# Attention in a two-block transformer kernel: projections cut in contraction halves and spread between the score blocks

## What is computed

```python
q = x @ Wq.T + bq + ocr_bias
k = x @ Wk.T + bk
v = x @ Wv.T + bv                      # 16 heads of 16 features each
scores = einsum('bhsd,bhtd->bhst', q, k) / sqrt(16)
scores = scores + band_mask            # 0.1 where |s - t| <= 2
attn = softmax(scores, axis=-1)
out = einsum('bhst,bhtd->bhsd', attn, v)
return out @ Wo.T + bo
```

## Time and profile before

| | us |
|---|---|
| median of 3 runs (lowest, highest) | 4187.68 (4182.49, 4190.27) |
| the profiled execution's own time | 4184.78 |
| its span, first to last instruction | 4183.0 |
| PE busy in the span | 3742.0 |
| attention loop, first to last first-pass maximum | 2157.3 to 3386.0 |

### The profile page before, as it was taken

One profiled execution on the slowest core, in us unless ns is written; L12 is line 12 of the kernel. 1 busy time (PEld: TensorE's weight loads), 2 busy tenths in 40 slices (PEclk: granted clock), 3 DMA queues, 4 the chain that ended last, 5 costly groups with the idle time before them and its releaser, 6 DMA issues. The chain is left out here.

```text
span 4183.0 us, 80084 instructions
## 1 busy us (share of the span) xinstructions
PE 3742.0 (89%) x27516; PEld 2902.7 (69%) x27516; DVE 2700.8 (65%) x5625; ACT 1772.3 (42%) x3205; POOL 1377.5 (33%) x1049
## 2 busy tenths in 40 slices
PE   6997788887997999999948998999998969999999
PEld 4886677776887888888824544555555538888888
DVE  5665677775666566666656666666666645666665
ACT  3444344443554333333325555555555553333333
POOL 2665222222665222222332333333323322222222
PEclk9999999998999899999969999999999989999999
DMA  3000000000001000000023323323323310000000
GB/s 102 0 0 14 2 0 0 0 0 1 0 0 38 1 0 0 0 0 0 1 72 88 88 68 87 87 68 88 86 68 91 83 46 6 15 10 10 15 10 16
DMA packets 92753, 131.72 MB, mean 31 GB/s; under 512 B 9824, under 2 KB 42992, under 8 KB 92672
## 3 DMA queue, kind: packets, MB, share of 16 engines
q1 hardware_dynamic: 90624, 130.13, 11.6%
q10 hardware_dynamic: 2048, 0.53, 0.1%
HBM read 71.38 MB, written 58.72 MB: 31 GB/s over the span
## 5 line engine op out<-in xcount | busy, mean ns | idle before, releaser
L1496 DVE TENSOR_REDUCE neg_max_sb<-s_ps 128x1 f32<-128x512 f32 x1024 | 667.3, 685 | 425.6 <-PE s_ps L1220 423.4
L1386 ACT ACTIVATE prob_sb<-s_ps 128x512 f32<-128x512 f32 x1024 | 575.0, 598 | 438.2 <-PE s_ps L1232 428.7
L850 POOL TENSOR_TENSOR m_act_lo_sb<-m_act_sb,m_act_hi_sb 128x512 fp32r<-128x512 f32 x320 | 414.2, 1295 | 1042.6 <-ACT m_act_hi_sb L816 1042.6
L806 ACT ACTIVATE m_silu_sb<-moe_h_ps 128x512 f32<-128x512 f32 x320 | 191.4, 598 | 967.4 <-PE moe_h_ps L761 967.4
L1138 POOL TENSOR_TENSOR prob_sb<-prob_sb,band_sb 128x520 f32<-128x520 f32 (+1 forms) x256 | 285.3, 1115 | 810.2 <-ACT prob_sb L1386 810.0
L904 DVE TENSOR_TENSOR m_act_sb<-moe_h_ps,m_silu_sb 128x512 f32<-128x512 f32 x320 | 220.6, 689 | 502.3 <-ACT m_silu_sb L806 472.7
L1232 PE MATMUL s_ps<-q_stack_sb,k_stack_sb 128*128 128x512 f32 x1024 | 409.1, 459 | 51.0 <-ACT prob_sb L1386 50.0
L529 POOL TENSOR_TENSOR f_sq_lo_sb<-f_sq_sb,f_sq_hi_sb 128x512 fp32r<-128x512 f32 x256 | 329.5, 1295 | 348.6 <-ACT f_sq_hi_sb L504 348.6
L1220 PE MATMUL s_ps<-k_stack_sb,q_stack_sb 96*128 96x512 f32 x1024 | 369.9, 430 | 71.7 <-DMA k_stack_sb<-qk_scratch 52.0
L916 DVE SCALAR_TENSOR_TENSOR x_resident_sb<-moe_y_ps,gates_sb,x_resident_sb 128x256 f32 (+1 forms) x1024 | 422.7, 475 | 0.5
L1232 PEld LDWEIGHTS s_ps<-q_stack_sb,k_stack_sb 128*128 128x128 f32 x1024 | 171.2, 191 | 359.5 <-ACT prob_sb L1386 212.3
(11 more groups left out here) (285 smaller groups left out, 8891.3 us busy)
## 6 DMA issues: line engine op xcount, KB each, us to landing
qk_scratch<-qk_hi_sb SPq DMA_DIRECT2D x128, 256.0 KB
q_stack_sb<-qk_scratch SPq DMA_DIRECT2D x128, 192.0 KB, 4.0
k_stack_sb<-qk_scratch SPq DMA_DIRECT2D x128, 192.0 KB, 4.2
qk_scratch<-qk_lo_sb SPq DMA_DIRECT2D x64, 256.0 KB
x_resident_sb<-x SPq DMA_DIRECT2D x4, 2048.0 KB, 17.7
out<-x_resident_sb SPq DMA_DIRECT2D x16, 512.0 KB
moe_w_values_sb<-routed_w SPq DMA_DIRECT2D x12, 512.0 KB, 6.5
q_stack_sb<-neg_max_t_sb ACTq DMA_DIRECT2D x128, 4.0 KB
```

The source lines that it names most:

```text
L850: nc.gpsimd.tensor_tensor(al[:, slot(e), :], act_f[:, e % 2, :], as_f32(ah[:, slot(e), :]), ALU.subtract).then_inc(low_ready, 1)
L1386: nc.scalar.activation(prob[:, kt % 2, i, :], s2p[i % 2][:, :], ACT.Exp).then_inc(exp_done, 1)
L1496: nc.vector.tensor_reduce(nm[:, g % 2, 2 * (i % 2) + i // 2, qt:qt + 1], s1p[n % 2][:, :], AXIS_X, ALU.max, negate=True).then_inc(max_done, 1)
```

## The change

The projections of tokens (v and the output) are cut in contraction halves: a piece is now three matmuls of 256 columns, so the tables have eight entries for each instead of four. All tables are rewritten, with the entries of DVE, ACT and POOL that follow from them: q and k of m = 1 are made at steps 5 and 6 instead of 8 and 9, the turning of the output goes from step 6 to step 7, the output projection from steps 10 and 11 to steps 8 to 11, the v projection from steps 13 to 15 to steps 12 to 15. `full` has a slice for each m, so m = 1 need not wait for `low_part` of m = 0. To make room, the spread value bias takes the place of `oh` and `ol`, which are used later. The number of instructions is the same. Score passes stay in blocks of two.

```diff
 XT_AT = [(1, 2), (2, 1)]
-QK_AT = [[(3, 2), (4, 0), (4, 1), (4, 2)], [(8, 0), (8, 1), (8, 2), (9, 0)]]
-OT_AT = [(6, 1), (6, 2)]
-Y_AT = [(10, 0), (10, 1), (10, 2), (11, 0)]
-V_AT = [(13, 2), (14, 1), (15, 0), (15, 2)]
+QK_AT = [[(3, 1), (3, 2), (4, 0), (4, 1)], [(5, 0), (5, 2), (6, 1), (6, 2)]]
+OT_AT = [(7, 0), (7, 1)]
+Y_AT = [(8, 1), (8, 2), (9, 0), (9, 2), (10, 1), (10, 2), (11, 0), (11, 1)]
+V_AT = [(12, 1), (12, 2), (13, 0), (13, 2), (14, 1), (14, 2), (15, 0), (15, 1)]
...
-        full = core.sbuf("qk_full", [P, 2, TOKENS], F32, ctx)
+        full = core.sbuf("qk_full", [P, KT, 2, TOKENS], F32, ctx)
...
-                        if more and st in (4, 9):
-                            low_part(b + 1, st // 8)
+                        if more and st in (4, 6):
+                            low_part(b + 1, int(st == 6))
...
-                def qk_proj(b, m, parts=range(4), after_o=False):
+                def qk_proj(b, m, parts=range(4)):
...
-                        if after_o:
-                            pe.wait_ge(ol_ready, b - 1)
...
-                def tokens(t, xh, xl, n, done):
-
-                    for k in range(KT):
-                        for i, (x, w) in enumerate([(xh, wh), (xh, wl), (xl, wh)]):
-                            op = nc.tensor.matmul(tpy[:, t, :], x[:, k, t * P:(t + 1) * P], w[n][:, k, :],
-                                                  start=(k == 0 and i == 0), stop=(k == KT - 1 and i == 2))
-                    if t == TILES - 1:
+                def tokens(piece, xh, xl, n, done):
+
+                    t, k = piece // KT, piece % KT
+                    for i, (x, w) in enumerate([(xh, wh), (xh, wl), (xl, wh)]):
+                        op = nc.tensor.matmul(tpy[:, t, :], x[:, k, t * P:(t + 1) * P], w[n][:, k, :],
+                                              start=(k == 0 and i == 0), stop=(k == KT - 1 and i == 2))
+                    if piece == TILES * KT - 1:
                         op.then_inc(done, 1)
...
-                                qk_proj(b + 1, 1, range(n, n + 1), before)
+                                qk_proj(b + 1, 1, range(n, n + 1))
                             if before and at in OT_AT:
                                 if more:
-                                    o_transpose(b - 1, OT_AT.index(at), full_ready, 2 * (KT * b + KT + 1))
+                                    o_transpose(b - 1, OT_AT.index(at), full_ready, 2 * (KT * b + 2 * KT))
...
-                    if not first(b) or m == 1:
-                        act.wait_ge(qkl_ready, KT * b + m)
-                    nc.scalar.activation(full[:, 1, :], tp[:, 1, :], ACT.Identity, bias=bk[:, m:m + 1]).then_inc(full_ready, 1)
+                    if not first(b):
+                        act.wait_ge(qkl_ready, KT * b + m - 1)
+                    nc.scalar.activation(full[:, m, 1, :], tp[:, 1, :], ACT.Identity, bias=bk[:, m:m + 1]).then_inc(full_ready, 1)
...
-                            if more and (st, i) in ((4, 3), (9, 1)):
-                                k_full(b + 1, st // 8)
+                            if more and (st, i) in ((4, 2), (6, 3)):
+                                k_full(b + 1, int(st == 6))
...
-                            if more and (st, i) in ((5, 1), (5, 2), (9, 2), (9, 3)):
-                                high_part(b + 1, st // 8, int((st, i) in ((5, 2), (9, 3))))
-                            if before and (st, i) in ((6, 3), (7, 0)):
-                                o_high(b - 1, st - 6)
+                            if more and (st, i) in ((4, 3), (5, 0), (7, 0), (7, 1)):
+                                high_part(b + 1, int(st == 7), int((st, i) in ((5, 0), (7, 1))))
+                            if before and (st, i) in ((7, 2), (7, 3)):
+                                o_high(b - 1, i - 2)
...
-                            if st % TILES == 2 and i == 3:
-                                if st > 2:
+                            if st % TILES == 3 and i == 2:
+                                if st > 3:
                                     normalise_out(b, st // TILES - 1)
...
-                            if more and (st, i) in ((4, 3), (9, 1)):
-                                q_full(b + 1, st // 8)
-                            if before and st == 7 and i in (0, 1):
-                                o_low(b - 1, i)
+                            if more and (st, i) in ((4, 2), (6, 3)):
+                                q_full(b + 1, int(st == 6))
+                            if before and (st, i) in ((7, 3), (8, 0)):
+                                o_low(b - 1, st - 7)
```

More of the change, by code:

```diff
@@ L1003, in att_stage @@
         oh, ol = (core.sbuf(n, [P, KT, TOKENS], F32R, ctx) for n in ("oh", "ol"))
-        ys = full[:, :, :].rearrange("p k (u d) -> p (k u) d", u=2)
+        bvs, bvl = oh[:, :, 0:P], ol[:, :, 0:P]
+        ys = full[:, 0, :, :].rearrange("p k (u d) -> p (k u) d", u=2)
         s1p = [core.psum(f"s1_{i}", [P, TOKENS], ctx) for i in range(2)]
@@ L1277, in o_transpose, with o_project @@
                         op.then_inc(o_ps, 1)
-                def o_project(b, t):
-                    if t == 0:
+                def o_project(b, piece):
+                    if piece == 0:
                         pe.wait_ge(ol_ready, b + 1)
-                    tokens(t, oh, ol, "o", y_ps)
+                    tokens(piece, oh, ol, "o", y_ps)
                 norm.transpose(pe, 0)
@@ L1286, in _ @@
                 qk_proj(0, 1)
-                for t in range(TILES):
-                    v_proj(0, t, False)
+                for piece in range(TILES * KT):
+                    v_proj(0, piece, False)
                 for st in range(AHEAD):
@@ L1347, in _ @@
                     o_transpose(last, k, *((y_ready, last + 1) if last else (v_ready, 1)))
-                for t in range(TILES):
-                    o_project(last, t)
+                for piece in range(TILES * KT):
+                    o_project(last, piece)
             @block.scalar
@@ L1353, in _ @@
                 act.wait_ge(spread, 1)
-                nc.scalar.copy(bvs[:, :, :], full[:, :, 0:P]).then_inc(spread_h, 1)
+                nc.scalar.copy(bvs[:, :, :], full[:, 0, :, 0:P]).then_inc(spread_h, 1)
                 norm.high(act, 0)
@@ L1375, in high_part @@
                             act.wait_ge(written[m], PER_WRITE * b)
-                    op = nc.scalar.copy(qkh[:, m, x, :], full[:, x, :])
+                    op = nc.scalar.copy(qkh[:, m, x, :], full[:, m, x, :])
                     if x:
@@ L1474, in _ @@
                 for k in range(KT):
-                    op = nc.vector.tensor_scalar(full[:, k, 0:P], core.ones[:, :], bv[:, k:k + 1], None, ALU.mult)
+                    op = nc.vector.tensor_scalar(full[:, 0, k, 0:P], core.ones[:, :], bv[:, k:k + 1], None, ALU.mult)
                 op.then_inc(spread, 1)
                 dve.wait_ge(spread_h, 1)
-                nc.vector.tensor_tensor(bvl[:, :, :], full[:, :, 0:P], as_f32(bvs[:, :, :]), ALU.subtract).then_inc(spread_done, 2)
+                nc.vector.tensor_tensor(bvl[:, :, :], full[:, 0, :, 0:P], as_f32(bvs[:, :, :]), ALU.subtract).then_inc(spread_done, 2)
                 dve.wait_ge(crow_ps, 1)
@@ L1486, in q_full @@
                     dve.wait_ge(qk_ps, KT * b + m + 1)
-                    if not first(b) or m == 1:
-                        dve.wait_ge(qkl_ready, KT * b + m)
-                    nc.vector.tensor_scalar(full[:, 0, :], tp[:, 0, :], bq[:, m:m + 1], SCALE, ALU.add,
+                    if not first(b):
+                        dve.wait_ge(qkl_ready, KT * b + m - 1)
+                    nc.vector.tensor_scalar(full[:, m, 0, :], tp[:, 0, :], bq[:, m:m + 1], SCALE, ALU.add,
                                             ALU.mult).then_inc(full_ready, 1)
```

12 lines of the change are left out of this document (5 added, 7 removed).

## The result

| | before | after |
|---|---|---|
| median us (lowest, highest), runs on one chip | 4186.51 (4182.49, 4190.27) | 4118.91 (4117.6, 4120.37) |
| ratio, 95% interval | | 0.9839 [0.9822, 0.9856] |
| the profiled execution | 4184.78 | 4119.09 |
| mean granted clock of TensorE | 0.968 | 0.972 |

The change takes 67.6 us off, 1.6%. The forecast was 4122.

The account below looks back on a forecast made before the run. PE was taken to bound the attention stage, at 3.06 us bare per step plus fillings and waits. Pieces -1.4 - 3.2 + 0.2 = -4.4 us per sequence, -61 in 14, -3 for the first: -64, forecast 4122, range 4085 to 4165.

Parts of the forecast that it names:

- The margin: At the first s1 of step 9, PE comes 0.9 us after the data of group 0, so its wait is gone.
- the first rival: Load keeps PE waiting at step 9: 1 us of wait and half a us of clock in 14 sequences, 4143; chance 0.15.
- The write of m = 1 behind load 1: This write, now directly behind the load, was taken to delay the data by nothing; bound 2.1 us later.
- Piece I: From `pv` in step 2 to the first s1 of step 9: 33.06 us becomes 31.7, gain 1.4 us per sequence.
- Piece II: From the first s1 of step 9 to `pv` in step 11: 14.03 us becomes 10.8, gain 3.2 us.
- Piece III: From `pv` in step 11 to `pv` in step 2 of the next sequence, 31.09 us before: +0.2 us.
- The term of `normalise_out`: Standing in step 11 ahead of `y_out` (0.25 + 0.42 us), it gives step 12 0.65 us more.
- The rule of the gaps: In a step, gap A has some 0.7 to 0.9 us free where ACT or DVE is behind; gap B has nothing free.
- Outside the 14 sequences: First sequence -3 us, last sequence 0, prologue 0.
- The new waits aren't there: Rival: transfer holds PE in piece I (30.8 us), piece III even or 0.7 better; 4097, chance 0.19.
- It does nothing: Rival: saving at step 9 comes back at steps 5, 8 and 12, 1.5 us more each; 4186, chance 0.06.
- The slower case: Rival: PE waits for ACT and DVE in steps 3, 5, 8, 12 and its clock falls; 4220, chance 0.1.

Follow-up runs that it names:

- early alone: Kernel before with only the q and k projection of m = 0 and its roundings at the new places; 4148.97 us, ratio 0.9911.
- the output pieces later: Changed kernel with whole v and output tiles, output roundings one to two units later and first output tile in step 9; 4109.07 us, ratio 0.9814.
- experiment 3: Kernel before with the issue of `max_row` for step 9 moved behind the second rounding of m = 1; 4168.79 us, ratio 0.9956.
- the first experiment: Changed kernel with `q_full`, `k_full` and roundings of m = 0 back where they were before; 4146.08 us, ratio 0.99.
- the whole tiles: Changed kernel with v and output tiles whole again (six matmuls), each in gap A; 4110.04 us, ratio 0.9822.
- the kernel with both edits: Kernel before with early q, k parts and roundings of m = 0, and `max_row` of step 9 issued behind the roundings of m = 1; 4133.58 us, ratio 0.9875.

## Why the prediction was right, point by point

- **The load of group 0 in time** was the main term, and the first two experiments show it from both sides: late again costs 27 us, early alone gains 37. A part of that is the clock, 10 us in the kernel before.
- **The margin.** "PE comes 0.9 us after the data": it comes 0.6 after at the median, and 0.2 in the sequence shown above (issue at 2659.76 plus 5.93 is 2665.7, the s1 is at 2665.88). The rounding ended 3.44 us after `pv` of step 4, not 3.2. "17.3 us from the rounding to the data" was read from one sequence, whose 11.40 from the rounding to the issue is the shortest of all; the median is 11.69 before and 11.65 after, so 17.6. Against that, PE's own way was 0.2 longer. Had the margin been another 0.6 less, the first rival would have come in. One sequence was too little for a term that decides.
- **The write of m = 1 behind load 1** was taken at nothing, as the row of landings had it. The Trainium skill ("DMA: Bandwidth & Descriptors", "Latency and other measured facts"), with its 2 us for access to HBM under high load, gave an estimate of up to 1.8 us more. The traces do not agree with so much: from issue to landing it is 5.81 us in the changed kernel and 5.76 with the output pieces later, with the write behind the load, against 5.81 without. The term of nothing was right. The reason given, that the load is ahead in the same queue, was not tested by itself.
- **Piece I**, 31.7 forecast and 32.03 measured. The three waits stand where they were put: step 3 (5.85, measured 5.93), step 5 (5.45, measured 5.60), step 8 (5.4, measured 5.48). A wait of 1 to 2 us for `ol` was expected, and it is 1.30; for `norm.low` 0.8 was expected, and it is 1.15. The start of this piece, 33.06, was one sequence again; the median before is 33.33, so the gain is 1.30, not 1.03, against 1.4 forecast.
- **Piece II**, "Sum 10.8, gain 3.2 us": the end, 10.81, is right, but the account of what it replaced is not whole. I named the clock after the idle stretch, the pieces in steps 9 and 10, and "ACT's backlog". The runs give, by the medians, 0.9 us for the load in time, and that is all clock (piece II is 13.11 in both kernels where the clock stays); 1.1 for the issue of `max_row` that stood ahead of ACT's roundings and so of PE's s2, which the prediction did not have; and 1.2 for what else was moved, by difference. The stall in ACT's queue went with the change because m = 1 is rounded in step 7 now, where no row is issued; the changed kernel still has 20.6 us of exponentials behind issues, which in step 10 PE does not wait for. I got the sum by building the steps as changed from bare times, which needs no account of what went. That the 14.03 of the one sequence read for before lay by the median of 14.01 was luck: the 14 range from 13.11 to 14.61.
- **The clock.** That it falls after waits of 2.3 us and more was right for most of the kernel before, but not a rule: of its 14 waits of 2.33 to 4.48 us, three were followed by a clock of 1.00. The first rival priced the clock at half a us for every sequence. In the kernel before it was 0.73 on the mean, in the first experiment 3 us in 14 sequences.
- **Piece III**: "+0.2" forecast. Measured it is -0.15, 30.94 us against 31.09, so this term had the wrong sign. Step 12 rose by 0.99, not 1.05, step 14 by 0.27, not 0.15, step 0 by nothing, not 0.15, and step 15 fell by 1.06, not 0.8. The term of `normalise_out` is confirmed at 0.63. The rule of the gaps (0.35 for a piece in gap B, nothing in a covered gap A) is confirmed in steps 9 and 13 alone; the other four steps of the whole tiles gave less.
- **Outside the 14 sequences**, 3 us forecast, 2 measured, and that it is so near is luck: 3.8 in the first sequence and 1.1 in the last and behind it, where nothing was forecast, less 3.0 us of scatter ahead of the stage.

The rivals: the load still waited for did not come (1.2 us besides the start), but it was nearer than I had it. "The new waits aren't there" fell. It took the transfer as the floor of piece I, at 30.8, and the kernel with the output pieces later shows such a floor, but at 31.37. "It does nothing" fell too, since steps 5, 8 and 12 came out at their forecast and not 1.5 us over it each. The slower case needed idle stretches of 2.3 us; the longest new one is 1.3, and the clock rose.

Not settled: why the same idle stretch of some 2.6 us is followed now by 0.57, now by 1.00 of clock; and how the 15 us between the kernel with both edits and the changed kernel divide among its remaining edits.

## What to carry to other kernels

Build the steps of the changed order from bare times and the waits you can name; a sum of savings misses stalls that were not seen. Read a term that decides by a fraction of a us from all its repetitions, since one sequence was 0.3 us off here. Where the clock falls in some repetitions only, compare those that kept it. And when a stall is taken out, look for the one that it hid: the wait for `ol` covered the transfer, and the wait for `norm.low` covered DVE. ACT's issue was not covered by the wait for k (its 19 us could be had with that wait in place); it stood in the table of waits from the start and was not read.
